# Graph-attention stage of a four-layer graph transformer: attention weights prepared earlier, two heads started inside the feature turn, rows of logits sent as two halves

## The reference, cut to what matters

```
# layer 0, feed-forward: 8 experts, the best two of each node, and a shared one
x = x + _L0_ffn_ref(_layernorm(x, axis=-1)[None], ...)[0]
xn = _layernorm(x, axis=-1)
# layer 1, graph attention with 8 heads of 96 features
h = (xn @ W1).reshape(n, heads, out_c)
al_s = jnp.einsum('nhc,hc->nh', h, a_src)
al_d = jnp.einsum('nhc,hc->nh', h, a_dst)
e = jax.nn.leaky_relu(al_s[src] + al_d[dst], 0.2)
m = jax.ops.segment_max(e, dst, num_segments=n)
ex = jnp.exp(e - m[dst])
z = jax.ops.segment_sum(ex, dst, num_segments=n)
out = jax.ops.segment_sum(h[src] * (ex / z[dst])[:, :, None], dst, num_segments=n)
```

## Time and profile before

| | |
|---|---|
| median of 3 runs | 3299.75 us (3291.88 to 3300.95) |
| the profiled execution: time | 3296.41 us |
| its span | 3294.6 us |
| mean granted PE clock | 0.958 |
| PE busy | 3065.6 us, 93% |
| DVE, POOL, ACT busy | 52%, 43%, 23% |

### The profile page before, as it was taken

The page is one execution under the profiler, slowest core; times in us unless marked ns, Lnnn a source line. Parts: engine busy times, 40 slices in busy tenths (PEclk is TensorE's granted clock), DMA queues, the critical chain, the costliest instruction groups (busy, mean ns, idle before and its releaser), DMA issues.

```text
span 3294.6 us, 38724 instructions
## 1 busy us (share of the span) xinstructions
PE 3065.6 (93%) x13979; PEld 2397.6 (73%) x13979; DVE 1713.4 (52%) x2808; ACT 754.8 (23%) x1333; POOL 1427.1 (43%) x1007
## 2 busy tenths in 40 slices
PE   8999899999999987898997989899999998989978
PEld 3577577888888884676776468578888886778858
DVE  7734699474556435636765546433344436641141
ACT  1043211232333212102244122211111103121222
POOL 2022287524544360563440045366666664536600
PEclk9999899899999998998998999999999999999987
DMA  2011266212222121222210232133333322213313
GB/s 82 15 48 44 91 192 222 70 43 68 75 72 66 58 82 40 87 86 64 66 58 10 71 112 72 45 93 99 96 95 95 95 86 67 72 48 100 96 32 132
DMA packets 92132, 259.35 MB, mean 79 GB/s; under 512 B 10431, under 2 KB 11071, under 8 KB 91716
## 3 DMA queue, kind: packets, MB, share of 16 engines
q1 hardware_dynamic: 80352, 219.45, 21.8%
q10 hardware_dynamic: 11652, 38.19, 3.5%
HBM read 256.03 MB, written 1.57 MB: 78 GB/s over the span
## 4 chain that ended last, share of the span: by engine, by line
PE 85%; DVE 9%; issue 3%; ACT 2%; DMA 0%; ACTq 0%; DVEq 0%
PE ps L429 22%; PE ps L433 22%; PE ps L434 22%; DVE aux L2004 3%; PE ps L909 2%; PE ps L537 1%; PE ps L531 1%; PE ps L1269 1%; PE ps L995 1%; PE ps L801 1%; PE ps L790 1%; PE ps L783 1%; PE ps L775 1%; DVE hot L2454 1%; DVE row L1814 1%
## 5 line engine op out<-in xcount | busy, mean ns | idle before, releaser
L367 POOL TENSOR_SCALAR w_hi<-raw 128x768 fp32r<-128x768 f32 x498 | 461.9, 928 | 1654.6 <-PE ps L429 1445.6
L370 POOL TENSOR_TENSOR w_lo<-raw,w_hi 128x768 fp32r<-128x768 f32 x498 | 973.6, 1955 | 41.5
L429 PE MATMUL ps<-H_hi,w_hi 128*128 128x512 f32 x804 | 319.9, 398 | 21.1 <-issue 11.6
L429 PE MATMUL ps<-A_hi,w_hi 128*128 128x512 f32 x780 | 309.2, 396 | 12.1 <-ACT scr L1594 12.1
L433 PE MATMUL ps<-H_lo,w_hi 128*128 128x512 f32 x804 | 316.6, 394 | 0.0
L434 PE MATMUL ps<-H_hi,w_lo 128*128 128x512 f32 x804 | 316.5, 394 | 0.0
L429 PE MATMUL ps<-B_hi,w_hi 128*128 128x512 f32 x720 | 292.2, 406 | 21.3 <-DVE B_lo L1798 15.2
L433 PE MATMUL ps<-A_lo,w_hi 128*128 128x512 f32 x780 | 305.7, 392 | 0.0
L434 PE MATMUL ps<-A_hi,w_lo 128*128 128x512 f32 x780 | 305.2, 391 | 0.0
L433 PE MATMUL ps<-B_lo,w_hi 128*128 128x512 f32 x720 | 283.3, 393 | 0.0
L434 PE MATMUL ps<-B_hi,w_lo 128*128 128x512 f32 x720 | 283.1, 393 | 0.0
(11 more groups left out here) (490 smaller groups left out, 5802.1 us busy)
## 6 DMA issues: line engine op xcount, KB each, us to landing
raw<-stream_dram SPq DMA_DIRECT2D x558, 384.0 KB, 3.1
w_ring<-w_dram ACTq DMA_DIRECT2D x45, 384.0 KB, 3.6
u_rows<-rows_dram ACTq DMA_DIRECT2D x8, 768.0 KB, 5.8
rows<-rows_dram ACTq DMA_DIRECT2D x7, 768.0 KB, 4.0
w_last<-w_dram ACTq DMA_DIRECT2D x9, 384.0 KB, 3.6
x<-x_dram ACTq DMA_DIRECT2D x1, 1536.0 KB, 9.4
out_dram<-x ACTq DMA_DIRECT2D x1, 1536.0 KB, 5.1
orf<-orf_dram ACTq DMA_DIRECT2D x6, 192.0 KB, 3.0
```

The costliest lines, as they stand in the source:

```text
L367: pool.tensor_scalar(w_hi[:, b // 3, b % 3], raw[:, b // 3, b % 3], 1.0, 1.0, ALU.mult, ALU.mult)\
L370: pool.tensor_tensor(w_lo[:, b // 3, b % 3], raw[:, b // 3, b % 3], w_hi[:, b // 3, b % 3], ALU.subtract)\
L429: mm = pe.matmul(o, wh, xh, start=first, stop=False, skip_group_check=True)
```

## The change

1. **W blocks.** Blocks 4 and 5 go to the memory of operand B (`head_f`), with semaphores of their own, and ACT issues their loads right behind the norm with no wait. DVE makes three blocks between `comb_n` and `comb_t`, and three in `beside(1)` of expert 0.
2. **Rows of logits.** DVE writes a high half and, with one more instruction, a low half of the target rows. PE spreads each row with two fp32r matmuls whose stationary operand is one column of the identity, read 128 times, in place of one float32 matmul with a prepared selector.
3. **Order.** PE's order is now: head rows 0, tile 0, targets, head rows 1, tile 1, head rows 2, tiles 2 and 3, head rows 3, tiles 4 and 5, product 0, head rows 4, tile 6, product 1, head rows 5, tile 7, then products 2 to 7 with head rows 6 and 7 behind products 2 and 3. ACT's order follows. Feature tiles 4 to 7 use banks 4 and 5 only. Two slope buffers serve all heads in place of four, and DVE inverts head h-3 behind the weights of head h, in place of h-2.

```diff
+            aux_r = sb("aux_r", [P, 4, N], F32R, s)
...
+        gat_set = aux_r[0:8, :, :]
-        e_slope = [lambda m: edge_w[1][:, m], lambda m: exp_1[m // 2][:, 4 + m % 2], lambda m: exp_02[0][:, m],
-                   lambda m: exp_02[1][:, m]]
-        slope_of = [0, 1, 0, 1, 2, 3, 0, 1]
+        e_slope = [lambda m: edge_w[1][:, m], lambda m: exp_1[m // 2][:, 4 + m % 2]]
...
+        def gat_w1(k):
+            return w1_ring[:, k] if k < 4 else head_f[k - 4][:, :, :].rearrange("p k n -> p (k n)")[:, 0:D]
...
-                    done(pe.matmul(ps[:, b], gat_sel[0:8, 4 * r + h % 4], aux[0:8, 2 + h // 4], start=True, stop=True), b, "act")
+                    pe.matmul(ps[:, b], ident_r[0:8, 4 * r + h % 4:4 * r + h % 4 + 1].to_broadcast([8, P]), gat_set[:, 2 + h // 4], start=True, stop=False)
+                    done(pe.matmul(ps[:, b], ident_r[0:8, 4 * r + h % 4:4 * r + h % 4 + 1].to_broadcast([8, P]), gat_set[:, h // 4], start=False, stop=True), b, "act")
...
-                        b = (0, 1, 4, 5)[t % 4]
+                        b = (0, 1, 4, 5, 4, 5, 4, 5)[t]
...
                 def beside_features(t):
-                    if t == 1:
+                    if t == 0:
                         gat_targets(1, 4)
-                    if t in (1, 2):
-                        gat_head_rows(t)
+                    if t in (0, 1, 3):
+                        gat_head_rows((1, 2, None, 3)[t])
+                    if t == 5:
+                        pe.wait_ge(act_to_pe, S.due(act_to_pe))
+                    if t in (5, 6):
+                        gat_product(t - 5)
+                        gat_head_rows(t - 1)
                 gat_features(beside_features)
-                gat_head_rows(3)
-                pe.wait_ge(act_to_pe, S.due(act_to_pe))
-                for h in range(GAT):
+                for h in range(2, GAT):
+                    if h == 4:
+                        pe.wait_ge(act_to_pe, S.due(act_to_pe))
                     gat_product(h)
-                    if h + 4 < GAT:
+                    if h < 4:
                         gat_head_rows(h + 4)
...
-                before = [u for u in range(h) if slope_of[u] == slope_of[h]]
-                if before:
-                    act.wait_ge(exps_merged, NT * (before[-1] + 1))
+                if h >= 2:
+                    act.wait_ge(exps_merged, NT * (h - 1))
...
                 norm(x, acc, A)
+                for k in range(4, KC):
+                    load_gat_w1(k)
...
-                for k in range(4, KC):
-                    act.wait_ge(w1_free, GAT_W1 + k - 2)
-                    load_gat_w1(k)
                 experts("experts0", 2)
...
                 gat_exps(0)
-                for u in range(2 * NT):
-                    gat_feature(u)
-                    if u in (1, 2):
-                        gat_exps(u)
+                gat_feature(0)
+                gat_exps(1)
+                gat_feature(1)
+                gat_exps(2)
+                gat_feature(2)
+                gat_feature(3)
                 mark(act_to_pe)
                 gat_exps(3)
-                for h in range(4, GAT):
-                    gat_exps(h)
-                    gat_scaled(h - 4)
-                for h in range(GAT - 4, GAT):
+                gat_feature(4)
+                gat_feature(5)
+                gat_exps(4)
+                gat_feature(6)
+                gat_scaled(0)
+                gat_exps(5)
+                gat_feature(7)
+                mark(act_to_pe)
+                for h in range(1, 3):
+                    gat_scaled(h)
+                    gat_exps(h + 5)
+                for h in range(3, GAT):
                     gat_scaled(h)
...
-                freed(dve.tensor_copy(aux[0:8, 2 + half], ps[0:8, b]), b)
+                S.step(dve.tensor_copy(gat_set[:, 2 + half], ps[0:8, b]))
+                freed(dve.tensor_tensor(gat_set[:, half], ps[0:8, b], gat_set[:, 2 + half], ALU.subtract), b)
...
-                combine(8, gate_s[:, 6], gate_s[:, 10])
-                experts("experts0", 2, 10.0, True, lambda n: gat_vectors((range(4), range(4, KC))[n]) if n < 2 else None)
+                combine(8, gate_s[:, 6], gate_s[:, 10], lambda: gat_vectors(range(3)))
+                experts("experts0", 2, 10.0, True, lambda n: gat_vectors(range(3, KC)) if n == 1 else None)
...
                     gat_weights(h)
-                    if h >= 2:
-                        gat_inverse(h - 2)
-                for h in range(GAT - 2, GAT):
+                    if h >= 3:
+                        gat_inverse(h - 3)
+                for h in range(GAT - 3, GAT):
                     gat_inverse(h)
```

More of the change, by code:

```diff
@@ L189, in build @@
         scr = sb("scr", [P, KC, N])
+        with ExitStack() as s:
+            aux_r = sb("aux_r", [P, 4, N], F32R, s)
         aux = sb("aux", [P, 4, N])
@@ L316, in build @@
         u_rows_in = [sem(f"u_rows_in{b}") for b in range(2)]
+        gat_w1_in = [sem(f"gat_w1_in{b}") for b in range(2)]
         w1_free, u_high, u_split = sem("w1_free"), sem("u_high"), sem("u_split")
@@ L1405, in load_gat_w1 @@
             def load_gat_w1(k):
-                act.dma_start(w1_ring[:, k % 4], t["w1"][GAT_W1 + k]).then_inc(w1_in[k % 4], 16)
+                act.dma_start(gat_w1(k), t["w1"][GAT_W1 + k])\
+                   .then_inc(w1_in[k] if k < 4 else gat_w1_in[k - 4], 16)
             def load_u_rows(h):
@@ L1449, in gat_feature @@
                 g, m = divmod(u, NT)
-                b = (0, 1, 4, 5)[u % 4]
+                b = (0, 1, 4, 5, 4, 5, 4, 5)[u]
                 act.wait_ge(tile_for["act"], S.due(tile_for["act"]))
@@ L1463, in gat_exps @@
                     e1 = act.activation(e_one[h % 4](m), ps[:, b], ACT.Exp, bias=al[:, 0, m, h:h + 1])
-                    e2 = act.activation(e_slope[slope_of[h]](m), ps[:, b + 1], ACT.Exp, bias=gat_v[:, 3, m, h:h + 1])
+                    e2 = act.activation(e_slope[h % 2](m), ps[:, b + 1], ACT.Exp, bias=gat_v[:, 3, m, h:h + 1])
                     if m < NT - 1:
@@ L2317, in gat_vectors @@
                         dve.wait_ge(rows_in, S.due(rows_in, 16))
-                    dve.wait_ge(w1_in[k % 4], (w1_loads(k % 4) + k // 4 + 1) * 16)
+                    dve.wait_ge(w1_in[k] if k < 4 else gat_w1_in[k - 4], (w1_loads(k) + 1) * 16 if k < 4 else 16)
                     for r in range(2):
                         product = flat[:, r * D:r * D + D]
-                        S.step(dve.tensor_tensor(product, w1_ring[:, k % 4], rows[:, r], ALU.mult))
+                        S.step(dve.tensor_tensor(product, gat_w1(k), rows[:, r], ALU.mult))
                         ins = dve.tensor_reduce(u_all[:, k, r * GAT:r * GAT + GAT], product.rearrange("p (h c) -> p h c", h=GAT),
@@ L2377, in gat_weights @@
                         dve.wait_ge(act_to_dve, S.due(act_to_dve))
-                        dve.scalar_tensor_tensor(out=e, in0=e, scalar=1.0, in1=e_slope[slope_of[h]](m), op0=ALU.min, op1=ALU.max)\
+                        dve.scalar_tensor_tensor(out=e, in0=e, scalar=1.0, in1=e_slope[h % 2](m), op0=ALU.min, op1=ALU.max)\
                            .then_inc(exps_merged, 1)
@@ L2426, in router_logits, with combine @@
                 freed(dve.tensor_copy(gate_s[:, 0, :, 0:n], ps[:, 7, 0:32].rearrange("p (m e) -> p m e", m=NT)[:, :, 0:n]), 7)
-            def combine(n, score, rank):
+            def combine(n, score, rank, beside=None):
                 mask, two, tmp = gate_s[:, 7, :, 0:n], gate_s[:, 8, :, 0:n], gate_s[:, 9, :, 0:n]
@@ L2440, in combine @@
                    .then_inc(dve_to_pe, 1)
+                if beside:
+                    beside()
                 dve.wait_ge(tile_for["dve"], S.due(tile_for["dve"]))
```

## The result

The changed kernel takes 3267.78 us (median of 10 runs, 3254.78 to 3276.16). The kernel before, run beside it, took 3294.24 (10 runs, 3276.12 to 3301.1). The ratio is 0.9917 with a 95% interval of 0.9893 to 0.9941, so 27 us are won, with 19 and 35 as the ends. A later set of the same changed kernel gave 3272.18 and 0.9921. Four of the ten executions of the changed kernel (3254.78 to 3259.72) and two of the ten of the kernel before (3276.12 and 3281.03) lie apart from the others, some 15 us under their median, so the medians and ratios of such sets move by several microseconds with how many of these executions they hold.

The account below looks back on a forecast made before the run. PE holds 85% of the chain that ended last, so its standing and poor work can be won: 9.5 (restart) + 0.5 (clock behind it) + 10.2 (`gnn1`) = 20.2 us off 3299.75 gives 3279.5, range 3270 to 3289.

Parts of the forecast that it names:

- Base: Whole kernel: the gains are subtracted from 3299.75 us, the median of three runs of the kernel before.
- Restart of the second turn: `ffn0`, expert 0: PE starts its second turn 8.7 to 10.3 us earlier, 9.5 taken; 10.3 if `sel_now` is undisturbed.
- Clock behind the restart: `ffn0`, after PE's wait: the 2.2 us lost to half clock may stay or vanish; 0.5 won taken, by an `ffn2` row.
- The moved block: `ffn0`, expert 0's second group: one more block, 3.9 us on DVE, costs nothing; without cover up to 4.
- Head rows as halves: `gnn1`: two fp32r matmuls per row take 0.91 us per head in place of 1.91; without that, 5.9 less gain.
- The order: `gnn1`, head rows to transposes: 10.2 us won, between 3.4 and 14.2, with waits and about 4 us of slow clock.
- Clean clock: Rival, chance 0.12: the poor work caused every slow spell; total 26.7 less the lock's 0.8, time 3274.
- The clock stays as bad: Rival, chance 0.18: in `gnn1` rows and order give only 3.4 us; total 13.4, time 3286.
- The halves save nothing: Rival, chance 0.05: in `gnn1` the halved head rows bring no saving; 5.9 us less, time 3285.4.
- Two of the last three together: Rival, chance 0.06: two of slow clock, unhidden DVE blocks and useless halves; 7 to 9 us won, no measurable change.
- DVE's blocks aren't hidden: Rival, chance 0.06: in `ffn0` six products each wait a POOL subtraction, 11.0 us; 6 us of gain lost, time 3285.5.
- Slower: Rival, chance 0.03: in `gnn1` PE's wait at `gat_targets(1)` halves the clock until product 7; 51.5 us lost, time 3331.

Follow-up runs that it names:

- `four_blocks`: The changed kernel with DVE making four W blocks between `comb_n` and `comb_t` in place of three; 3282.29 us, one execution.
- `rows_twice`: The changed kernel with each pair of head-row halves sent twice into the same bank; 3287.59 us, ratio 0.9984 to the kernel before.
- `rows_128`: The changed kernel with head-row matmuls reading 128 rows, the lower 120 zero, in place of 8; 3275.41 us, ratio 0.9915 to the kernel before.
- `rows_128_twice`: The changed kernel with each pair of halves sent twice and these matmuls reading 128 rows; 3283.94 us, one execution.
- `only_order`: The kernel before with only the new order, its banks and slope buffers; head rows stay float32; 3279.82 us, ratio 0.9968.
- `rows_and_order`: The kernel before with the head rows as halves and the new order, W blocks as before; 3286.85 us, ratio 0.9961.
- `only_rows`: The kernel before with only the head rows as fp32r halves, sent in the old order; 3288.65 us, ratio 0.9982.

## Why the prediction was right and where it was wrong

The time came out below the range because three terms of the sum were mis-sized, all to the same side: the base, part A's restart, and the clock behind it. The mechanism of both parts was right, with errors inside part B that cancel.

1. **Base (wrong).** The sum of gains was subtracted from 3299.75, the median of three runs, on the ground that the forecast is for the median. The kernel before has medians of 3294.24, 3296.62, 3296.55, 3297.7 and 3297.48 in five larger sets (the first takes in the three). Against the one beside which the change was timed the base was 5.5 us too high, more than the 2.2 by which the range missed. Whether the median fell inside the range or not was luck: two sets of the changed kernel differ by 4.4 us. The profiled execution's own forecast, 3276.2, came out at 3271.52, 4.7 off.
2. **Restart of the second turn (size wrong).** 9.5 was taken, 10.6 came: 12.7 against 2.1 us behind T. The laid-out table was nearly right: the third block was to end 17.0 us after the first began and ended after 16.2. What was mis-sized is the step "the copy of `sel_now` may wait once more, up to 1.8", for which 0.8 was charged. The copy does wait for POOL's subtraction, as the prediction says, but here it lost almost nothing. With no POOL instruction beside it, it takes 0.55 (`four_blocks`); in the changed kernel it took 0.61, and before 0.97, and in both it ended 0.41 behind the end of POOL's subtraction:

```profile
1330.74 0.55 DVE L2305 COPY sel_now<-sel 16x768 f32<-16x768 f32 x1
```

```profile
1320.31 1.81 POOL L375 TENSOR_TENSOR w_lo<-raw,w_hi 128x768 fp32r<-128x768 f32 x1
```

   So the row from which the undisturbed gain of 10.3 was read held 0.4 us of this wait already, and in the changed kernel the subtraction happened to be near its end: that part of the gain is luck. PE idled 1.5, not the 1.9 to 3.5 forecast. The Trainium skill ("SBUF — State Buffer", "Who interferes with whom") has DVE's operations on two SBUF inputs and POOL's lock each other out, and reductions never; the trace agrees, with 2.40 against 0.96 for the products, 1.55 against 0.83 for POOL's high halves, and 0.95 for every reduction. By it, a block more would not have fitted, and `four_blocks` shows that it doesn't.
3. **Clock behind the restart (size wrong).** 0.5 of 2.2 was taken by the row of `ffn2`; the whole 2.1 came. `ffn2` was not the right place to compare with. There PE spreads a row with 16 rows behind its short wait before any full matmul, in `ffn0` the turn itself follows. The profile of before shows the former so:

```profile
2151.46 1.12 PE L863 MATMUL ps<-comb_t,sel_now 16*128 16x512 f32 x2 [1.44 <-DVE sel_now L2286]
```

   It still stands in the changed kernel, with a clock of 0.50 from 2126.2 to 2129.7. But the same wait (1.44 to 1.49) and the same 16 rows are followed by 0.50 in eleven of the fourteen profiles and by 1.00 alone in three (`rows_twice`, `rows_128`, `rows_128_twice`), so neither decides it by itself. In `ffn0` the clock stayed at 1.00 in all nine profiles with a short wait. Why the two places differ wasn't tried; the 16 rows are a likely part, by the runs with 8 and 128 rows.
4. **The moved block (right).** The third column shows 0.4 us less, not more, and its spread among kernels is 0.9: a third block beside the additions cost PE nothing that shows.
5. **Head rows as halves (gain right, size of a set wrong).** The repeated column did no harm, 0.23 us from start to start. But "0.91 us per head in place of 1.91" is four such steps without the two ends of a set, and by the same measure as the 1.91 it was 1.12. What the halves are worth came out as said, 5.9: the rows alone gave 5.7 us to the stage, and without them, in `only_order`, it takes 80.3 - 74.4 = 5.9 more. The prediction doesn't show how its 5.9 was worked out; eight sets at 1.0 each would be 8.
6. **The order (total right, by errors that cancel).** 10.2 was forecast, 10.7 came in the stage. Work at full clock is 62.4 us by the prediction's sum. It put waits of 2.6, 1.5, 2.2 and 1.9 on top, 8.2, and 4 us of half clock. The waits were 4.5. The clock was 0.50 for 3.4 us in tile 0 and 6.9 in product 4, which costs half of that, 5.1. The other 2.4 us are work that the sum had too small: matmuls of 8 rows between those of 128 rows, 1.9 us for five sets of head rows, by which eight would cost 3.0 (an estimate from the two windows above). In the kernel with 128 rows the sum closes: 62.4 of work, 8.9 of waits and 1.7 for the clock (0.50 for 3.4 us) are 73.0 of 73.2. The wait of 2.6 at the targets was 0.45 because tile 0 in front of it ran at half clock for 3.4 us; with tile 0 at 1.00 it was 2.0 in `rows_and_order` and 2.2 with 128 rows. What the prediction missed is that half clock, slower work and waits are not added but hide each other.
7. **Rivals.** *Clean clock* is true of part A and of the cause, not of the result: poor work was the cause of most slow spells, but taking it away wholly gave 1.3 us. *The clock stays as bad* (a stage near 82) is refuted by the 74.4, *The halves save nothing* by `only_order`, which takes 5.9 us more, and with them *Two of the last three together*. *DVE's blocks aren't hidden* is refuted by 1.5 us of waiting, though three of six products did wait for POOL, 1.4 us each. *Slower* never began: the longest stretch at a low clock in the stage is product 4's 7 us.

In sum: 5.5 us of the 11.7 between forecast and median are the base, 2.7 are part A up to the spread row (12.7 against 10.0), 0.4 are the third column, 0.5 part B (10.7 against 10.2). The other 2.6 lie within the interval of the ratio, and nothing in the stages answers to them.

## What to carry to other kernels

Subtract a sum of gains from many runs of the kernel before, not from three, and let the range hold the error of that base as well as those of the terms. Before a blocked engine is moved ahead, ask what stands behind it: memory alone moved the wait from one instruction to another for nothing, and memory with an earlier place for the work won 13 us. When a clock spell and a wait follow each other on the same engine, price them as one: each of them covers a part of the other, and curing either returns little as long as another engine (here ACT and DVE, the latter beside POOL) sets the pace. Price a new form of matmul between its neighbours and not only among its like: the head rows cost 0.2 us a set more than four of their steps.

## What was not expected of the hardware

- A matmul that reads few rows lets the granted clock fall while PE is recorded as busy all the time: 0.82 to 0.84 in three successive windows with 8 rows sent twice, 1.00 at the same times with 128 rows, for as many matmuls of the same columns in the stage, and 10.4 us of difference in a stage of 88. Four matmuls of 16 rows stand in front of the only fall with 128 rows that has no wait before it.
- In `ffn0` PE restarted at 1.00 behind 1.5 to 1.8 us of standing (nine profiles), at 0.50 for 4.5 us behind 7.6, 9.6 and 12.1. In `ffn2`, behind 1.44 to 1.49, the clock fell to 0.50 in eleven profiles and stayed at 1.00 in three, with the same instructions.
- At full clock, a set of four matmuls of 8 rows between matmuls of 128 rows costs PE 0.38 us more than the same set with 128 rows (39.79 against 37.90 us for five sets).
- DVE's copy of `sel_now` from SBUF to SBUF, with one input, waits for POOL's subtraction: 0.55 us alone, 0.61 and 0.97 beside one, and 1.42 for the next expert in the kernel before, each time ending 0.41 behind the subtraction's end.
- With an fp32r stationary operand that is one column read 128 times, matmuls of 512 columns start 0.23 us apart, like those with a full one.
- Parts of the program with the same instructions take 1320.3 to 1328.6 us at its beginning and 1524.1 to 1542.9 at its end, from profile to profile. For the shortest end, that of `only_order`, the traces say where it comes from. Near the end PE makes 192 matmuls of 64 columns and 128 rows, with no wait among them, at half clock in `only_rows` (first line) and at full clock in `only_order`:

```profile
3217.54 38.72 PE L1273 MATMUL ps<-exp,raw 128*128 128x64 f32 x192 [1.01 <-ACT junk L1305]
```

```profile
3219.14 21.91 PE L1272 MATMUL ps<-exp,raw 128*128 128x64 f32 x192 [1.01 <-ACT junk L1304]
```

  They take 36.0 to 41.2 us in the other thirteen profiles, at a mean clock of 0.50 to 0.63, and 21.9 at 1.00 in this one. So matmuls of 128 rows too can go on at half clock for some 40 us while PE is recorded as busy. What decides the level there stays open, and so does the cause of the 8 us at the beginning.
